# One attention and expert layer on one core: the experts' stage taken by pairs of tiles

## The reference

```python
xn = layernorm(x)
# attention, 16 heads of 16, with rotary positions
qkv = einsum('bld,ed->ble', xn, w_qkv)
attn = softmax(einsum('blhd,bmhd->bhlm', rope(q), rope(k)) / 4)
s = einsum('bld,ed->ble', einsum('bhlm,bmhd->blhd', attn, v), w_out)
# experts: each row to the one with the largest logit
expert_idx = argmax(einsum('th,eh->te', xn, gate_w))
g = einsum('th,ehd->etd', xn, wg)          # 256 -> 64
u = einsum('th,ehd->etd', xn, wu)          # 256 -> 64
inter = square(relu(g)) * u * onehot
y = einsum('etd,edh->th', inter, wd)       # 64 -> 256
return x + s * silu(y)
```

## Time and profile before

| | |
|---|---|
| median of three runs | 1469.42 us |
| lowest and highest | 1468.78 and 1470.99 us |
| the profiled execution's own time | 1468.86 us |
| its span | 1467.1 us |
| PE busy | 1443.2 us (98%) |
| DVE busy | 1341.5 us (91%) |
| ACT busy | 1193.1 us (81%) |
| POOL busy | 161.9 us (11%) |
| granted TensorE clock | 0.999 of full speed |

### The profile page before, as it was taken

The page is one execution under the profiler, slowest core; times in us unless marked ns, Lnnn a source line. Parts: engine busy times, 40 slices in busy tenths (PEclk is TensorE's granted clock), DMA queues, the critical chain, the costliest instruction groups (busy, mean ns, idle before and its releaser), DMA issues.

```text
span 1467.1 us, 32004 instructions
## 1 busy us (share of the span) xinstructions
PE 1443.2 (98%) x11201; PEld 649.0 (44%) x11201; DVE 1341.5 (91%) x1979; ACT 1193.1 (81%) x2381; POOL 161.9 (11%) x221
## 2 busy tenths in 40 slices
PE   7999999999999999999999999999999999999988
PEld 5655444444485444444444444444444444444326
DVE  6689999999946999999999999999999999999806
ACT  3653488898867998898988988888888988899990
POOL 5333322300001221000010000000010000000110
PEclk9999999999999999999999999999999999999999
DMA  5875243326354456333232343333323522333323
GB/s 180 275 208 146 63 85 84 78 38 124 50 175 106 83 86 127 56 49 48 43 48 42 48 101 44 47 47 49 48 46 45 104 46 42 45 49 48 71 70 119
DMA packets 79801, 119.55 MB, mean 81 GB/s; under 512 B 28962, under 2 KB 66210, under 8 KB 72738
## 3 DMA queue, kind: packets, MB, share of 16 engines
q1 hardware_dynamic: 73714, 105.82, 36.4%
q0 software_dynamic: 3072, 8.39, 2.3%
q10 hardware_dynamic: 2896, 3.62, 0.7%
HBM read 77.15 MB, written 39.71 MB: 80 GB/s over the span
## 4 chain that ended last, share of the span: by engine, by line
PE 94%; ACT 2%; DVE 1%; DMA 1%; issue 1%; SPq 0%; POOL 0%; ACTq 0%; POOLq 0%
PE ps L1244 39%; PE ps L1258 36%; PE ps L1232 5%; PE ps L1160 3%; ACT arena L659 2%; PE ps L1438 2%; PE ps L1161 1%; PE ps L1391 1%; PE ps L1193 1%; PE ps L1375 1%; PE ps L1185 1%; PE ps L1172 1%; PE ps L1342 1%; PE ps L1137 0%; PE ps L1384 0%
## 5 line engine op out<-in xcount | busy, mean ns | idle before, releaser
L1232 PE MATMUL ps<-ks,qs 48*128 48x512 f32 x1984 | 687.1, 442 | 0.0
L1244 PE MATMUL ps<-qs,ks 50*128 50x512 f32 x2048 | 677.1, 434 | 0.5 <-ACT arena L663 0.3
L810 DVE TENSOR_REDUCE arena<-ps 128x1 f32<-128x512 f32 x992 | 639.0, 682 | 6.9 <-PE ps L1232 6.7
L659 ACT ACTIVATE arena<-ps 128x512 f32<-128x512 f32 x1056 | 566.4, 605 | 77.0 <-PE ps L1244 64.4
L813 DVE TENSOR_REDUCE arena<-ps 128x1 f32<-128x1024 f32 x496 | 604.4, 1219 | 0.6 <-PE ps L1232 0.6
L659 ACT ACTIVATE x_sb<-ps 128x512 f32<-128x512 f32 x992 | 535.1, 598 | 58.3 <-PE ps L1244 41.0
L1244 PEld LDWEIGHTS ps<-qs,ks 50*128 50x128 f32 x2048 | 326.6, 184 | 473.9 <-issue 173.1
L1232 PEld LDWEIGHTS ps<-ks,qs 48*128 48x128 f32 x1984 | 323.9, 184 | 11.1 <-issue 3.0
L1258 PE MATMUL ps<-arena 128*32 128x256 f32 (+1 forms) x3104 | 307.6, 468 | 5.7 <-ACT arena L659 4.1
L1258 PE MATMUL ps<-x_sb,arena 128*32 128x256 f32 (+1 forms) x2960 | 290.2, 464 | 0.0
L1258 PEld LDWEIGHTS ps<-arena 128*32 128x32 f32 x3104 | 62.3, 107 | 125.0 <-issue 125.0
(11 more groups left out here) (116 smaller groups left out, 624.7 us busy)
## 6 DMA issues: line engine op xcount, KB each, us to landing
qs<-parts_d SPq DMA_DIRECT2D x186, 128.0 KB, 4.5
ks<-parts_d SPq DMA_DIRECT2D x186, 128.0 KB, 5.1
parts_d<-arena SPq DMA_DIRECT2D x64, 256.0 KB, 2.8
xs_d<-arena SPq DMA_DIRECT2D x13, 384.0 KB, 3.5
arena<-xs_d SPq DMA_DIRECT2D x13, 384.0 KB, 3.9
ys_d<-arena SPq DMA_DIRECT2D x13, 384.0 KB, 2.8
x_sb<-in_x SPq DMA_DIRECT2D x2, 2048.0 KB, 12.9
onum_d<-arena SPq DMA_DIRECT2D x124, 32.0 KB, 1.6
```

The source lines that it names most:

```text
L659: nc.scalar.activation(prob_of(pi, s, kb)[:, c * W:(c + 1) * W], ps[:, bank, :], ACT.Exp, scale=SCALE).then_inc(exp_done[bank], 1)
L810: nc.vector.tensor_reduce(most[head_slot][:, tile, u:u + 1], ps[:, AB + lo, :], AX.X, ALU.max).then_inc(a_reduced[u], 1)
L1232: ins = nc.tensor.matmul(ps[:, AB + c, :], qs[head_slot][ABASE:ABASE + KR, tile * P:(tile + 1) * P].bitcast(F32R), ks[head_slot][ABASE:ABA ...
L1244: nc.tensor.matmul(ps[:, bank, :], ks[s][at:at + KS, kb * P:(kb + 1) * P].bitcast(F32R), qs[s][at:at + KS, c * W:(c + 1) * W].bitcast(F32R ...
```

## The change

The experts' stage goes by pairs of tiles j (tiles 2j and 2j+1; `NF2` is 20).

- PE's round j is: turn tile 2j+2, gate and up of tile 2j, turn tile 2j+3, gate and up of tile 2j+1, one transpose of `inter` of pair j-1, then the two down matmuls of pair j-2. `inter` now holds an even tile in columns 0 to 63 and an odd one in 64 to 127, so one transpose and one copy (DVE) serve both. The even tile's down matmul reads partitions 0 to 63 alone, the odd one's partitions 64 to 127 alone.
- The down weights are loaded twice, to both halves of the partitions (two transfers more). For the odd tile GpSimd copies its expert's 64 x 256 block to one of two fixed places (`stage_down`, 19 copies), two pairs ahead. The zero fills of `wd2` and `inter` go.
- The turned tiles have two banks and four buffers (before: one and two). Small buffers move into `turn`, which is free by then.
- ACT's round j is: silu of tiles 2j-6 and 2j-5, then copy, relu, copy, relu.
- SP issues the load of group g+3 before the store of group g-2 (before: of group g).
- PE reads the five expert words in steps 2 to 6 of the head before the stage, and not in the stage.
- The last tile's result goes to bank 0. PE makes four of the first scores of head pair 3 ahead of that tile's down matmul, and ACT runs a one-element exponential right behind the last silu.

```diff
@@ SP: experts @@
                     if g + XR < NF // FG:
                         load_sorted(g + XR)
+                    if g >= 2:
+                        store_sorted(g - 2)
+                for g in range(NF // FG - 2, NF // FG):
                     store_sorted(g)
@@ ACT: experts @@
+                for j in range(NF2 + 3):
+                    for i in (2 * j - 6, 2 * j - 5):
+                        if 0 <= i < NF:
+                            act.wait_ge(y_done, i + 1)
...
+                            nc.scalar.activation(ysb[g % XR][:, z, :], ps[:, y_bank(i), 0:D], ACT.Silu).then_inc(y_out, 1)
+                    for i in (2 * j, 2 * j + 1):
+                        if i + 2 < NF:
+                            turned_out(i + 2)
+                        if i < NF:
+                            act.wait_ge(hid_done, i + 1)
+                            if i >= 2:
+                                act.wait_ge(inter_ready, i - 1)
+                            nc.scalar.activation(hr[i % 2], ps[:, EB + i % 2, 0:DE], ACT.Relu).then_inc(relu_done, 1)
+                nc.scalar.activation(table_in[:, 1:2], table_in[:, 0:1], ACT.Exp)
@@ DVE: experts @@
+                        nc.vector.tensor_tensor(inter[j % 2][:, i % 2 * DE:(i % 2 + 1) * DE], hu[i % 2], hr[i % 2],
                                                 ALU.mult).then_inc(inter_ready, 1)
...
+                    if j >= 1:
+                        dve.wait_ge(inter_turned, j)
+                        if j >= 3:
+                            dve.wait_ge(y_done, 2 * (j - 2))
+                        nc.vector.tensor_copy(interT[(j - 1) % 2], ps[:, PVB, 0:P]).then_inc(inter_out, 1)
@@ POOL @@
+            def stage_down():
+
+                pool.wait_ge(expert_ready, 1)
+                pool.wait_ge(expert_weights, 16 * 8)
+                pool.wait_ge(v_staged[1], FB + 1)
+                for i in range(1, NF, 2):
+                    g, z = divmod(i, FP)
+                    if z == 1:
+                        packed = pool.value_load(expert[0:1, g:g + 1], min_val=0, max_val=E ** FP - 1)
+                    which = pool.snap(packed // E ** z % E, min_val=0, max_val=E - 1)
+                    if i >= 4:
+                        pool.wait_ge(y_done, i - 3)
+                    if i > 1:
+                        pool.wait_ge(down_staged, i // 2)
+                    nc.gpsimd.tensor_copy(down_up[i // 2 % 2][DE:P, :].unsqueeze(1),
+                                          wd2[DE:P, bass.ds(which, 1), :]).then_inc(down_staged, 1)
@@ PE: pair @@
+                        if hold and s == 1 and 2 <= kb <= 1 + NE // FP:
+                            if kb == 2:
+                                pe.wait_ge(expert_ready, 1)
+                            load_word(kb - 2)
@@ PE: experts @@
+                for j in range(NF2 + 2):
+                    for i in (2 * j, 2 * j + 1):
+                        if i + 2 < NF:
+                            turn_sorted(i + 2)
...
+                    if 1 <= j <= NF2:
...
+                        nc.tensor.transpose(ps[:, PVB, 0:P], inter[(j - 1) % 2], ident[:]).then_inc(inter_turned, 1)
+                    if j == NF2 + 1:
+                        open_heads()
+                    if j >= 2:
...
+                        elif j <= NF2:
+                            pe.wait_ge(y_out, 2 * (j - 2))
+                        pe.wait_ge(inter_out, j - 1)
+                        for i in (2 * j - 4, 2 * j - 3):
...
+                            if i % 2:
+                                pe.wait_ge(down_staged, i // 2 + 1)
+                                rows, weights = slice(DE, P), down_up[i // 2 % 2][DE:P, :]
+                            else:
+                                rows, weights = slice(0, DE), wd2[0:DE, bass.ds(which[i], 1), :]
...
+                pe.wait_ge(y_out, NF)
+                score(FB, 0, 0, 0)
+                for c in range(2, QT):
                     score_a(FB * (2 * KB) + AHEAD, 1, AHEAD - KB, c)
```

More of the change, by code:

```diff
@@ L45, in layer_kernel, with y_bank @@
     FG = 3
-    TB, EB, YB = 0, 1, 6
+    TBS, EB, YB = (0, 5), 1, 6
+    def y_bank(i):
+        return YB + i % 2 if i < NF - 1 else TBS[0]
+    XB = 4
     XR = 3
@@ L156, in layer_kernel @@
         xs = [cut([FG, D]) for _ in range(XR)]
-        xsT = [cut([KC, P]) for _ in range(2)]
-        hr = [cut([DE]) for _ in range(2)]
-        hu = [cut([DE]) for _ in range(2)]
+        xsT = [cut([KC, P]) for _ in range(XB)]
         inter = [cut([P]) for _ in range(2)]
@@ L173, in layer_kernel @@
         res_at = at[0]
+        down_up = [turn[:, i * 8:(i + 1) * 8, :].rearrange("p t w -> p (t w)") for i in range(2)]
+        hr = [turn[:, 16 + 2 * i:18 + 2 * i, :].rearrange("p t w -> p (t w)") for i in range(2)]
+        hu = [turn[:, 20 + 2 * i:22 + 2 * i, :].rearrange("p t w -> p (t w)") for i in range(2)]
         prob = [cut([L]) for _ in range(2)]
@@ L475, in load_experts @@
                                      src[:, k, :].rearrange("p (e f) -> p e f", f=DE)).then_inc(expert_weights, 16)
-                for i in range(2):
-                    sp.dma_start(wd2[0:DE, :, :].rearrange("p (c i) d -> p c i d", i=2)[:, :, i, :],
-                                 wd_in[i * DE:(i + 1) * DE, :, :]).then_inc(expert_weights, 16)
+                for half in range(2):
+                    for i in range(2):
+                        rows = wd2[half * DE:(half + 1) * DE, :, :].rearrange("p (c i) d -> p c i d", i=2)
+                        sp.dma_start(rows[:, :, i, :], wd_in[i * DE:(i + 1) * DE, :, :]).then_inc(expert_weights, 16)
             def experts():
@@ L910, in experts @@
             def experts():
-                for i in range(NF + 1):
-                    if i < NF:
+                for j in range(NF2 + 1):
+                    for i in (2 * j, 2 * j + 1):
+                        if i >= NF:
+                            continue
                         dve.wait_ge(relu_done, i + 1)
@@ L1357, in open_experts, with open_heads @@
                     pe.wait_ge(exp_done[b_bank(FB - 1, 1, KB - 1, c)], past(b_before(FB - 1, 1, KB - 1, c) + 1))
-                pe.wait_ge(expert_ready, 1)
-                expert_of(0)
                 turn_sorted(0)
[L1362 to L1392, removed]
-                    if i + 1 < NF:
-                        expert_of(i + 1)
-                pe.wait_ge(inter_out, NF)
-                spin(1, PVB)
+            def open_heads():
                 pe.wait_ge(loaded[0], (FB + 1) * (16 * LOADS))
```

93 lines of the change are left out of this document (50 added, 43 removed).

## The result

The changed kernel takes 1458.32 us in the median of four runs (1457.91 to 1460.06), the kernel before, run beside it, 1469.72 (1468.78 to 1470.99). The ratio is 0.9914, 95% interval 0.9893 to 0.9934. The profiled execution took 1457.91 us, 10.95 less than the one before.

What follows compares the result with a forecast made beforehand. PE was taken to bound the stage, with a loop adding about 0.2 us a tile. Stage and seams save 11.9 us, less 1.0 in the head: 10.9, giving 1458.0 to 1458.5, stated as 1458.2; 8-in-10 range 1451.5 to 1465.0.

Steps and rivals of the forecast that it cites:

- The stage and its seams: Experts' stage with its start and tail: 11.9 us less, at 2.27 us a pair of tiles against 2.83 before.
- The tail: From the last tile's gate and up to the first exponential: 5.3 us, against 5.43 before.
- Full overlap of the down pair: Two down matmuls on different row halves run together on PE: 0.43 us, against 0.86 without overlap.
- no overlap: Rival: the two down matmuls do not overlap, costing 7.7 us, 1466 us; chance 0.22 together with half overlap.
- half an overlap: Rival: the second down matmul's first pass runs beside the first's second, 1462 us; chance 0.22 together with no overlap.
- The change of split: PE going between whole array and halves, twice a pair of tiles: 0.4 us a pair, bounds 0 and 0.48.
- The loop: In the stage before, PE, ACT, DVE, PE wait in a ring that adds about 0.2 us a tile; pairs cut it.
- A pair much under 2.2: Rival: a shorter pair, lower bound 1.88 us if changing the array's split costs nothing; chance of a shorter time 0.15.
- Expert words in the head: Five word reads moved into the head before the stage cost 1.0 us, bounds 0 and 4; first turn 0.4 earlier.
- GpSimd: Its copies of down weights take 0.4 to 1.3 us a pair, hidden under the 4.5 us allowed: price 0.
- the rival's rule: Rival: GpSimd sets the pace if its work exceeds a pair's 2.27 us; slower than before from 2.84; chance 0.06.
- SP: Loads, 3.8 us to land and 0.5 to issue, asked for 7.9 us after they may go: price 0.

Runs made afterwards that it cites:

- E4: The changed kernel with the odd tile's down matmul on the same half of the rows as the even one; one run, 1464.71 us.
- E3: The changed kernel with both down matmuls over all 128 rows of the array; 1460.82 us, 0.9937 of before.
- E1: The kernel before, without pairs, with DVE's copy of tile i-1 moved ahead of its multiplies for tile i; 1463.76 us, 0.9959 of before.
- E6: The changed kernel with PE reading the five expert words in the stage as before; one run, 1456.73 us.
- E9: The changed kernel with each of GpSimd's 19 copies of down weights made six times, one waiting for the other; one run, 1480.3 us.
- E7: The changed kernel with SP issuing load g+3 ahead of store g again, not of store g-2; one run, 1479.43 us.
- E2: The changed kernel with one more filler matmul behind the last down matmul; 1457.93 us, 0.9912 of before.
- E5: The changed kernel with the four early scores of head pair 3 behind the last down matmul again; 1458.92 us, 0.9925 of before.

## Why the prediction was right

1458.2 us was forecast and 1458.32 measured. The mechanism was right, but a good part of that closeness is luck. Term by term, in the trace's own time:

- *The stage and its seams:* forecast 11.9 us less, measured 11.8 (0.38 + 2.03 + 10.44 - 1.07). The pair was forecast at 2.27 and is 2.22, which is 0.8 us over 16 rounds. The tail ran the other way. From the last tile's gate and up (439.74) to the first exponential (445.63) it takes 5.89 us for 5.3 forecast (the terms as listed add to 5.24), and 0.4 of it is the wait of the down pair of tiles 36 and 37 for the silus of 34 and 35, which I had not seen.
- *Full overlap of the down pair:* right, E4. The rivals "no overlap" and "half an overlap" fell.
- *The change of split:* right in size, 0.36 for 0.40, and E3 shows that it eats three quarters of what the overlap gives. The rule of the Trainium skill, page "TensorEngine Tiling (Array Packing)", section "Key Properties", that a change of the tiling mode drains the TensorE, agrees with the trace as far as start times can tell. The price here was about 0.1 us each way, and 0.1 and 0.06 again on the next start.
- *The loop:* right, E1 shows it in the kernel before, and in the changed one no copy is waited for in the middle of the stage. Of the 0.2 us a tile that I gave to the loop, E1 takes away 0.13; some of the rest are the word reads. A pair much under 2.2 was not seen either: with a down matmul over the whole array behind it (E3) the transpose takes 0.10 to the next start, so there was nothing in it to hide the change of split behind.
- *Expert words in the head:* the step "I take 1.0, near the low end" was wrong in size: 0.07 us. I took the sequencer's time for the array's. That the first turn starts 0.4 earlier was right. By E6 the other four reads would cost nothing in the stage either, once the pairs are there.
- *GpSimd:* right, 0.40 us a copy; E9 shows the rival's rule (the pace is GpSimd's time for a pair once that is over PE's).
- *SP:* the step "Price 0" was right for the change as a whole and hid what matters most. I priced the loads in the new order, and never the pairs in the old one: 20.4 us (E7). Of all the parts it is the one that the gain stood or fell with.
- *Not forecast:* half clock behind the stage, +1.4 us, and a start of the heads that is 0.58 us earlier. The latter is not shown to be the change's: the same stretch took 153.07 and 154.52 us in two profiles of the changed kernel, and 153.65 and 153.09 in two with the front part of the kernel before.

The words (0.93 too dear) and the early start (0.58) together cancel the missed clock (1.42 too cheap) to within 0.1 us. The one-element exponential and the added banks and buffers were not tried alone. No version measured is shown to be faster than the changed kernel: E2 and E6 lie within its runs' spread or one run below it; E5 shortens the tail by 0.35 us in the trace, below what the runs can tell.

## What to carry to other kernels

Where an engine looks full, take start-to-start times of one round: if rounds alternate (1.21 and 1.52 here), look for an operation that another engine holds behind later work; moving that one line may give a good part of a rewrite's gain. A deeper pipeline moves each release later in the round; go through every in-order queue, the one that issues transfers above all, and ask which load now stands behind a store that waits. Splitting the array has a price for each change of the split, to be set against what the overlap between two changes saves. For 256 columns in two passes it was nearly a draw, 0.42 us won and 0.33 paid; longer stretches were not tried.

## What the runs showed of the hardware

- Two matmuls of two passes each, on partitions 0 to 63 and 64 to 127, ran pass beside pass, started 10 ns apart; four passes took 0.64 us to the next start, 1.06 on one half.
- The change of split cost 0.36 us for one stay on the halves, once in and once out: four passes on one half started 0.32, 0.22 and 0.22 us apart and the next whole-array matmul 0.31 behind.
- The granted clock fell to 0.50 for some microseconds in single executions of kernels whose PE reads as 98% busy, at different places (173.7 and 173.9, 444.7, 450.7, 1391.6 and 1392.0 us), at a price of 1.2 to 1.6 us where it was read; what decides the place stays open. In E9 it lasted 17 us. Runs of the kernel before with a mean clock of 0.999 were 2.5 us and more faster than those with 0.996 or less.
- A read of a word into PE's registers cost 0.40 us at the stage's start and nothing in the middle of the pairs. In the one-tile order the rounds at the four reads were 1.8 us longer in sum.
- DVE's multiply with both inputs in the on-chip buffer, started in the first 0.22 us of a GpSimd copy, ended 0.07 to 0.08 us behind the copy (up to 456 ns for 224). The multiply with one input in PSUM kept its 221 ns (E9).
